# Routing and shared expert of a two-layer transformer block: weight split moved into attention and to GpSimd, barrier ahead of the experts taken out, order of the work between written out

## What is computed

```
x = x + tanh(g_xattn[0]) * xattn0(layernorm(x), ctx)   # 16 heads, "stablemax" for softmax
x = x + tanh(g_ffn[0])   * moe(layernorm(x))           # 64 experts, top 8, capacity 128, shared expert
x = x + tanh(g_xattn[1]) * xattn1(layernorm(x), ctx)   # 16 heads, softmax
x = x + tanh(g_ffn[1])   * ffn1(layernorm(x))          # 256 -> 1024, butterfly, gelu, butterfly, 1024 -> 256
```

```python
gu = x @ shared_gate_up_w                               # 256 -> 2 * 512
shared = _silu(gu[:, :Is]) * gu[:, Is:] @ shared_down_w
shared = shared * jax.nn.sigmoid(x @ shared_gate_w)
logits = x @ gate_w                                     # 64 experts
w, idx = jax.lax.top_k(jax.nn.softmax(logits), 8)       # renormalised over the 8
pos = ...cumsum(onehot) - 1                             # place of a token in its expert's list
y = experts(buf)[e_flat, slot] * w_flat                 # dropped where pos >= 128
return (y + shared)
```

## Time and profile before

| | |
|---|---|
| three runs | 1160.8, 1161.38, 1163.43 us, median 1161.38 |
| the profiled execution | 1164.33 us, its span 1162.5 us |
| PE busy | 995.5 us (86%) |
| DVE busy | 790.7 us (68%) |
| ACT busy | 623.9 us (54%) |
| POOL busy | 384.8 us (33%) |
| DMA | 128 MB, 110 GB/s over the span |

### The profile page before, as it was taken

How to read it: one execution, slowest core, us unless ns; L and a number is a source line. 1 busy time by engine, 2 the same in 40 slices (tenths; PEclk the granted TensorE clock), 3 DMA queues, 4 the chain that set the end, 5 groups by cost and what they waited for, 6 DMA issues and landing times.

```text
span 1162.5 us, 16849 instructions
## 1 busy us (share of the span) xinstructions
PE 995.5 (86%) x5379; PEld 711.7 (61%) x5379; DVE 790.7 (68%) x2003; ACT 623.9 (54%) x1205; POOL 384.8 (33%) x385
## 2 busy tenths in 40 slices
PE   4899899899756889988999858889898889989988
PEld 2355455555445778876878636456666666757657
DVE  4679998998777577556576476876766677564443
ACT  1877788878454245555554222655554455454632
POOL 6000010100000137787677420242425252504234
PEclk9899999999878899999999966899999999999999
DMA  6728455451314338889887443312321323110000
GB/s 141 208 60 221 135 165 165 106 148 51 109 55 149 102 83 183 212 196 256 188 181 176 95 117 100 78 58 68 88 75 50 99 70 93 28 49 1 21 19 19
DMA packets 101559, 128.38 MB, mean 110 GB/s; under 512 B 31136, under 2 KB 73504, under 8 KB 101216
## 3 DMA queue, kind: packets, MB, share of 16 engines
q1 hardware_dynamic: 87088, 106.32, 32.1%
q0 software_dynamic: 12288, 18.88, 9.1%
q10 hardware_dynamic: 2096, 2.10, 0.8%
HBM read 66.15 MB, written 30.70 MB: 83 GB/s over the span
## 4 chain that ended last, share of the span: by engine, by line
PE 53%; DVE 26%; ACT 9%; issue 6%; POOL 3%; DMA 1%; ACTq 1%; SPq 1%; DVEq 0%; POOLq 0%
PE psum L969 6%; PE psum L1153 5%; PE psum L1138 5%; PE psum L1058 4%; PE psum L985 4%; DVE weights L1561 3%; PE psum L876 3%; PE psum L847 3%; DVE peaks L1852 3%; PE psum L922 2%; DVE stats L1425 2%; PE psum L871 2%; PE psum L1085 2%; PE psum L1017 2%; PE psum L793 2%
## 5 line engine op out<-in xcount | busy, mean ns | idle before, releaser
L1951 POOL TENSOR_SCALAR vareps<-moments 128x4 f32<-128x4 f32 x32 | 12.1, 379 | 438.1 <-DVE moments L1435 438.1
L847 PE MATMUL psum<-q_stack,k_stack 97*128 97x512 f32 (+1 forms) x256 | 120.8, 497 | 20.0 <-DVE weights L1561 7.9
L1359 ACT ACTIVATE weights<-psum 128x512 f32<-128x512 f32 x160 | 92.9, 595 | 66.1 <-PE psum L847 58.2
L1971 POOL DMA_INDIRECT expert_sums<-made,sum_rows x64 | 104.7, 1636 | 60.6 <-DVE made L1816 41.5
L1085 PE MATMUL psum<-k_stack,q_stack 96*128 96x308 f32 x256 | 86.2, 397 | 36.5 <-DVE peaks L1852 25.0
L1561 DVE SCALAR_TENSOR_TENSOR weights<-weights,psum 128x512 f32<-128x512 f32 x160 | 102.8, 678 | 13.3 <-ACT weights L1214 13.0
L1852 DVE TENSOR_REDUCE peaks<-psum 128x2 f32<-128x308 f32 x256 | 105.6, 468 | 7.5 <-PE psum L1085 7.3
L1209 ACT ACTIVATE weights<-psum 128x512 f32<-128x512 f32 x160 | 89.6, 595 | 27.3 <-PE psum L847 27.3
L2003 POOL TENSOR_TENSOR hidden<-hidden_whole,hidden 128x512 fp32r<-128x512 f32 x64 | 82.8, 1298 | 62.1 <-DVE hidden L1900 62.1
L969 PE MATMUL psum<-feat_parts,w_shared_up 128*128 128x512 f32 x384 | 97.9, 405 | 5.1 <-DVE shared_silu L1690 2.6
L1153 PE MATMUL psum<-w_con_high,hidden 128*128 128x256 f32 x512 | 100.8, 296 | 0.5 <-POOL hidden L2003 0.5
(11 more groups left out here) (211 smaller groups left out, 2229.8 us busy)
## 6 DMA issues: line engine op xcount, KB each, us to landing
expert_w<-in_expert_w SPq DMA_DIRECT2D x64, 384.0 KB
q_stack<-q_stage SPq DMA_DIRECT2D x96, 128.0 KB, 2.4
q_stack<-q_stage SPq DMA_DIRECT2D x174, 64.0 KB, 2.0
expert_sums<-zeros SPq DMA_DIRECT2D x6, 1408.0 KB, 7.9
fetched<-expert_sums SPq DMA_DIRECT2D x14, 512.0 KB, 4.6
...
```

The source lines that it names most:

```text
L847: T.matmul(to, keys_of(h, head), q[0:row, head // 2, :], start=True, stop=True).then_inc(scored, 1)
L1359: A.activation(weights1[n % 6][:, :], score_bank[n % 2], ACT.Exp).then_inc(exped, 1)
L1971: G.indirect_dma_start(sum_dram[e % SUMS], bass.IndirectOffsetOnAxis(ap=sum_rows[:, e:e + 1], axis=0), made[e % 4][:, :], None, bounds_che ...
```

## The change

- **No barrier ahead of `experts`.** The five engines meet only ahead of `last`. What the barrier ordered has waits of its own: the first `gather` waits for the stores and the cleared sums, `sh_weights` for what lies in the bytes of the shared weights, `load_expert(0)` for the four splits.
- **The shared weights are fetched and split during the last half of attention.** `sh_fetch` stands twelve chunk sets ahead of the end and `sh_weights` six. `shared_staging` lies in other bytes, where half 5's queries and keys were.
- **The four subtractions go from DVE to POOL**: `sh_weights` in attention, `sh_split(0)` ahead of `norm(r,7)`'s second part in the plan.
- **The order behind the last chunk is a string**, `TAIL`. Each letter issues one unit: `l` one of `late`, `s` one of `back`, `h` a table, `p` a placing, `t` `lists`. All 32 tables and placings and `lists` now stand in `first`. `ranks(6)` comes ahead of the first table, no shared step stands within half 7's routing, and `lists` comes after 10 of the shared steps.
- `count(7)` has no DVE part (its sums went to nobody). Loads of the butterfly's inputs and of the first three experts are issued behind `gate_weights(1)`. `spare_row` and `diag` come with the other constants.
- The tables `Q_AT`, `K_AT`, `A_AT` and `R_AT` change by a slot here and there. They act in all eight halves.

```diff
-AHEAD = 3
-TAIL_TILES = 18
-SHARED_AT, SHARED_EARLY = (6, 13, 14), 4
+WEIGHTS_AT = (6,)
+TAIL = 'lhhlplhllhlhplphllhphlllphlplsplllhhphplpphlhhpllplplphphphhlhllshphsphpsphshpphshpphhpshsphphpspsppts'
...
-Q_AT = (-34, -26, -24, -21, -21, -20, -19, -19, -17, -17, -17, -16, -16)
-K_AT = (-16, -15, -8, -7, -6, -5)
-A_AT = (24, 25, 25, 26, 25, 26, 25, 26, 26, 27, 28, 30, 29, 30)
-R_AT = (33, 33, 33, 35, 35, 37, 38, 38, 40, 40, 41, 42, 43, 44, 49)
+Q_AT = (-34, -25, -24, -21, -21, -20, -19, -19, -17, -17, -17, -16, -16)
+K_AT = (-19, -18, -15, -7, -6, -5)
+A_AT = (24, 25, 25, 26, 25, 26, 25, 26, 26, 27, 27, 30, 29, 30)
+R_AT = (33, 33, 33, 35, 35, 36, 38, 39, 40, 40, 40, 42, 43, 44, 50, 54)
...
+        if i == len(sets) - 12:
+            plan.append(("sh_fetch",))
         if i == len(sets) - 6:
             plan.append(("load_hots",))
+        if i == len(sets) - WEIGHTS_AT[0]:
+            plan.append(("sh_weights",))
...
             for n, plan in enumerate((first, experts, last)):
-                if n:
+                if n == 2:
                     T.drain().then_inc(stage_over, 1)
-                    T.wait_ge(stage_over, 5 * n)
+                    T.wait_ge(stage_over, 5)
...
             def sh_weights():
                 A.wait_ge(sgu_in, 16)
+                A.wait_ge(keys_split, BATCH)
+                A.wait_ge(*misc.freed(("values", BATCH - 1)))
+                wait_all(A, k_in[(BATCH - 1) % 2], BATCH // 2)
+                A.wait_ge(weighed, 2 * GROUPS * (HALVES - 2))
...
+            def sh_weights():
+                for n in range(2):
+                    part = slice(n * 2 * SHARED, (n + 1) * 2 * SHARED)
+                    G.wait_ge(sh_rounded, n + 1)
+                    G.tensor_tensor(w_sgu[:, 1, part], sgu_staged[:, part], w_sgu[:, 0, part].bitcast(F32),
+                                    ALU.subtract).then_inc(sh_split, 1)
+
+            def sh_split_(h):
+                if h == 0:
+                    G.wait_ge(sh_rounded, 3)
+                    G.tensor_tensor(sh_parts[:, 1], sh_feats[:, :], sh_parts[:, 0].bitcast(F32),
+                                    ALU.subtract).then_inc(sh_split, 1)
+                    G.wait_ge(sh_rounded, 4)
+                    G.tensor_tensor(w_sd[:, 1], sd_staged, w_sd[:, 0].bitcast(F32),
+                                    ALU.subtract).then_inc(sh_split, 1)
...
             def load_expert(e):
+                if e == 0:
+                    S.wait_ge(sh_split, 4)
...
             def sh_fetch():
-                S.wait_ge(weighed, 2 * KEPT1)
+                S.wait_ge(scored, PER_HALF * (HALVES - 2))
+                wait_all(S, q_in[(HALVES - 1) % 2], HALVES // 2)
                 S.dma_start(sgu_staged, D["w_sgu"]).then_inc(sgu_in, 16)
                 S.dma_start(sd_staged, D["w_sd"]).then_inc(sd_in, 16)
-                S.wait_ge(feats_out, 16)
```

143 lines of the change are left out of this document (67 added, 76 removed).

## The result

The changed kernel takes **1143.36 us** (median of 4 runs, 1143.01 to 1145.61), the kernel before 1162.26. The ratio is 0.9839, 95% interval 0.9825 to 0.9852: 18.9 us faster. The forecast was 1146.2 with a range of 1139 to 1153. The profiled execution took 1145.61, its span is 1143.8.

What follows compares the result with a forecast made beforehand. Attention fills PE and DVE, experts PE; the tail between, a chain to the row numbers, was the loose part. Tail -22.4, experts +5.7, attention +1.5 give -15.2: 1161.38 to 1146.2 us, range 1139 to 1153.

Steps and rivals of the forecast that it cites:

- Slot tables: All eight halves of attention: the changed order of units, with no row to price it, taken 0, bounds -3 and +3.
- rival 5: Attention: moved key or query units keep a PSUM bank from the next chunk; at 2.5 us per half, 1166; chance 0.05.
- Conversions in attention: Attention: ACT's two copies cost +1.1 and half 6's `rstd` comes some 1.5 late; together +1.5, bounds 0 and 4.
- `turn_att` to `x_add`: Tail leg of 8.53 us, to the end of `x_add`: same units in the same order on PE, 0.
- To the end of `norm`: Tail leg of 13.30 us behind `x_add`: two tables and the four conversions leave, -7.7, to 5.6.
- The routing: Leg `highest` to `gate_weights`, 17.86 us: DVE loses shared products and `count` sums, gains a table; -4.7, to 13.2.
- To the lists: Leg from `gate_weights` to the end of `lists`, 36.2 us: barrier's hole goes, shared steps come in; 29.8, -6.4.
- The low clock: Behind `gate`: PE may fall to the low clock, first `sh_up` taking twice as long (+2.8); half expected, +1.4.
- Rival 2: Behind the routing: two of six `sh_up` at half clock, +5.6 instead of +1.4, 1150.4; chance 0.11.
- Experts: One deferred `sh_up` and one `sh_down` of half 1 paid at full PE price: +2.8 + 2.9 = +5.7, bounds 0 and 8.
- Rival 1: POOL's subtractions hold DVE's tables: +1.9 behind `rstd`, up to +2 in attention, 1150.1; chance 0.13.
- Rival 4: Tail: a unit in the string waits on another engine, tail behind `norm` stays as long but for the barrier; 1150 to 1153; chance 0.08.

Runs made afterwards that it cites:

- one-sided runs: Kernel before with only the four slot tables changed: 1157.16 us, ratio 0.9955; changed kernel with the old slot tables: 1148.11 us, ratio 0.9871.
- five_deferred: Changed kernel with five more shared steps (both `sh_down` of half 0, `sh_up(1,0)`, the two behind it) moved among the experts: 1150.91 us, ratio 0.9907.

## Why the prediction held, step by step

Forecast -15.2, measured -18.9. At the row numbers it had 20.9 us less (-22.4, and +1.5 in attention); the profile shows 401.16 and 380.41, **20.75 less**. The agreement there is luck to a good part, since two large misses cancel. Of the other 3.5 us, 2.4 are the experts, which grew by less than forecast, and 1.2 the last stage, which is within its scatter. By step:

- **Slot tables, taken 0, bounds -3 and +3:** -1.6 up to half 0's gate and -1.0 to half 5's in the profiled pair. Both one-sided runs confirm the sign, with 2 to 3 us by stretches and 4 to 5 by whole times; which of the two is right stays open. This is the largest miss in the attention part; rival 5, which let the tables cost 1.9 per half, had the sign wrong.
- **Conversions in attention, +1.1 on ACT and what `rstd` lost, 1.5 in all:** half 5's gate to half 6's went from 29.16 to 29.85, so +0.7; with the old tables 29.35, so +0.2. Over-sized.
- **First table to `turn_att`, -1.5:** from half 6's gate to `turn_att` 12.70 became 10.87, -1.8. (In the changed order `ranks(6)` stands ahead of the first table, so I measure from the gate.)
- **`turn_att` to `x_add`, 0:** 8.5 became 9.9. "The same units in the same order on PE" was true and not enough: on DVE `hots(7)`, which waits for a placing, had come ahead of `x_add(7,1)`. A step that names one engine's order must look at the other's as well.
- **To the end of `norm`, -7.7:** 13.3 became 9.6, -3.7. The step that failed. The conversions left ACT and DVE as told, but POOL's subtractions began 0.17 ahead of `norm` and held it, +3.9.
- **To the gate, 0:** -0.8. Of this 0.6 is the clock: the gate's matmuls took 2.47 us before and 1.90 after, since the low clock ended earlier in them.
- **The routing, -4.7:** 17.9 became 13.4, -4.5. DVE was busy 13.1, the forecast 12.7 and 0.5 for waits.
- **To the lists, -6.4:** the hole went, and the leg is 5.3 shorter. (The prediction read `lists` as 2.1 us, up to 390.30, but the row that begins at 389.67 lasts 1.22: `lists` takes 2.66 and ended at 390.89. With that mark the leg went from 36.7 to 31.4, as the window of the changed kernel ends with `lists`. The slip moves 0.6 from this leg to the next and leaves the forecast difference as it was.) So 1.1 are missing. (By the prediction's own price of 0.80 for two, its 15 placings make 6.0, not 6.5.) PE's waits in the leg, for ACT and DVE, are all ahead of 356.59 (0.54, 0.68, 0.33 and 0.64 us); from there to the last placing it had none. The loads that the prediction took "at nothing", with up to 2 if late, were late: issued at 348.93 behind nine others, with the copy at 356.83, not near 353. ACT waited 1.02 for them and DVE 1.46 behind that, but PE was in the two `sh_down` meanwhile, and it was held only when these were taken away (`five_deferred`).
- **Lists to row numbers, -3.5:** with the same mark 10.3 became 6.6, -3.7.
- **The low clock, +1.4:** the first `sh_up` took 3.05 us, so this was not paid. The routing and the stretch to the end of `norm` ran at 0.87 and 0.61, the placings at 1.00. Rival 2 did not come, but it was near: in three of the other orders an `sh_up`, two `sh_down` or the gate's matmuls fell into the low clock and cost 1.5 to 1.9.
- **Experts, +5.7:** +3.3 in the profiled pair to the last plan, +3.1 as means over ten and two profiles (263.8, 260.6). The price for one step, 2.8, is borne out (2.3 to 2.9 for each of five). That some fall into PE's idle time, the lower bound, is what the run with one more step showed for the first of them.

**Rival 1** (POOL holds DVE, +3.9) was right as a mechanism and wrong in its victim and its parts. It had priced 1.9 for the tables behind `norm` and up to 2 in attention. What was held was `norm`: 3.9 on its own leg, and nothing that could be seen in attention. How much of it reaches the gate depends on what takes its place: 0.8 was won back with the tables held instead, 1.1 with tables held earlier and the gate's matmuls at half clock, 2.6 with the subtractions on DVE. It still didn't bring 1150, because the gain of the slot tables, at 0 in the forecast, came in on the other side. Of the forecast the `norm` leg was 4.0 too hopeful and attention 3.7 too dark; the other misses ahead of the row numbers, 0.2 to 1.4 each, cancel as well. Rival 4 is out, the written order did what it said.

The Trainium skill ("SBUF — State Buffer", section "Who interferes with whom") says that a DVE operation with at most one SBUF input doesn't contend with GpSimd, outside the two-port modes, and also that `tensor_scalar` can enter such a mode. `norm` is a `tensor_scalar` with one tensor in SBUF. The runs agree with the second half: two of its operations were held, 2.33 and 2.43 us for 0.41. Applied only to work with two inputs in SBUF, as the prediction applied it in rival 1, the rule points at the tables and misses `norm`. Whether `norm`, with two scalars per partition, runs in the two-port mode no run here shows.
